# Eight graph layers on one core: batch norm folded into the next attention layer, staged stores moved between copies, a shorter last group

## What is computed

```python
def _gat_conv(x, src, dst, ea, W, a_src, a_dst, We, a_edge, bias):
    ...
    alpha = leaky_relu(al_s[s] + al_d[d] + al_e, 0.2)
    ...
    coef = ex / (denom[d] + 1e-16)
    out = segment_sum(h[s] * coef[:, None], d, num_segments=n)
    return out + bias
def _bn(x, gamma, beta):
    mu = x.mean(0)
    var = ((x - mu) ** 2).mean(0)
    return (x - mu) * rsqrt(var + EPS) * gamma + beta
```

## Time and profile before

| what | value |
|---|---|
| median of 3 runs | 9399.09 us (9398.47 to 9403.84) |
| the profiled execution's own time | 9414.12 us |
| its span in the profile | 9412.4 us |
| POOL busy | 6368.0 us, 68% of the span |
| DVE busy | 5206.9 us, 55% |
| PE busy | 4490.4 us, 48% |
| ACT busy | 1396.4 us, 15% |
| mean granted PE clock | 0.647 of full speed |
| gathers of table rows | 6272 |

### The profile page before, as it was taken

One profiled execution on the slowest core, in us unless ns is written; L12 is line 12 of the kernel. 1 busy time (PEld: TensorE's weight loads), 2 busy tenths in 40 slices (PEclk: granted clock), 3 DMA queues, 4 the chain that ended last, 5 costly groups with the idle time before them and its releaser, 6 DMA issues.

```text
span 9412.4 us, 97859 instructions
## 1 busy us (share of the span) xinstructions
PE 4490.4 (48%) x25775; PEld 3609.4 (38%) x25775; DVE 5206.9 (55%) x15729; ACT 1396.4 (15%) x2273; POOL 6368.0 (68%) x6626
## 2 busy tenths in 40 slices
PE   0655556666433344333533357254374552672533
PEld 0444433333433344333433354253352442542533
DVE  3587567777433343333433349585376763695844
ACT  1666654434200000000100020000000000100001
POOL 0777747777677767777677747777557777377774
PEclk9877777777656566555656555576655765656756
DMA  2455547776211222111211112332123321123311
GB/s 73 149 156 156 154 149 199 203 200 190 76 52 52 53 57 53 52 52 52 57 53 52 52 52 77 114 116 59 24 66 110 119 79 39 58 87 103 112 52 28
DMA packets 596438, 855.81 MB, mean 91 GB/s; under 512 B 130149, under 2 KB 400236, under 8 KB 594928
## 3 DMA queue, kind: packets, MB, share of 16 engines
q0 software_dynamic: 211680, 414.97, 17.1%
q1 hardware_dynamic: 369708, 383.31, 13.1%
q10 hardware_dynamic: 14688, 53.48, 1.4%
HBM read 654.55 MB, written 196.72 MB: 90 GB/s over the span
## 4 chain that ended last, share of the span: by engine, by line
POOL 66%; issue 23%; PE 4%; DVE 3%; SPq 1%; DMA 1%; ACT 1%; POOLq 0%; ACTq 0%; DVEq 0%
POOL rows L730 39%; POOL rows L760 23%; POOL nd L743 2%; POOL at_first L736 2%; SPq L516 1%; PE PS L1041 1%; PE PS L1015 1%; PE PS L1049 1%; DMA rows<-table,src_t 1%; POOL acc L777 0%; ACT H L817 0%; PE PS L1076 0%; PE PS L1079 0%; DMA staged<-rows 0%; DVE H L1641 0%
## 5 line engine op out<-in xcount | busy, mean ns | idle before, releaser
L730 POOL DMA_INDIRECT rows<-table,src_t x3920 | 3736.8, 953 | 1678.9 <-issue 1258.4
L1458 DVE TENSOR_TENSOR acc<-acc,PS 128x128 f32 x5488 | 1558.2, 284 | 3013.8 <-PE PS L1127 1768.8
L760 POOL DMA_INDIRECT rows<-table,src_t x2352 | 2287.7, 973 | 1129.5 <-issue 758.0
L1127 PE MATMUL PS<-onehot,rows 128*128 128x128 f32 x6272 | 1426.6, 419 | 2288.2 <-DMA rows<-table,src_t 2288.2
L1127 PEld LDWEIGHTS PS<-onehot,rows 128*128 128x128 f32 x6272 | 1320.0, 320 | 2448.2 <-DMA rows<-table,src_t 2448.2
L1158 PE MATMUL PS<-onehot,rows 128*128 128x128 f32 x3072 | 681.9, 412 | 1196.1 <-DMA rows<-table,src_t 1128.7
L1158 PEld LDWEIGHTS PS<-onehot,rows 128*128 128x128 f32 x3072 | 630.3, 313 | 1241.4 <-DMA rows<-table,src_t 1183.6
L1538 DVE TENSOR_SCALAR onehot<-PS,loc_t,shared 128x128 f32<-128x128 f32 x2352 | 943.7, 403 | 0.5
L1440 DVE TENSOR_TENSOR onehot<-PS,loc_t 128x1024 f32<-128x1024 f32 x392 | 476.8, 1217 | 0.4
L830 ACT ACTIVATE rows<-acc 128x128 f32 x343 | 77.7, 296 | 2688.5 <-DVE acc L1458 2686.4
L1231 PEld LDWEIGHTS PS<-als_bf,onehot 128*128 128x128 bf16 x7056 | 308.2, 119 | 426.5 <-DVE onehot L1712 269.6
(11 more groups left out here) (314 smaller groups left out, 5912.8 us busy)
## 6 DMA issues: line engine op xcount, KB each, us to landing
rows<-table,src_t POOLq DMA_INDIRECT x6272
staged<-rows ACTq DMA_DIRECT2D x102, 512.0 KB
H<-staged SPq DMA_DIRECT2D x102, 512.0 KB, 3.6
soft_rows<-shared SPq DMA_DIRECT2D x196, 256.0 KB
H<-soft_rows SPq DMA_DIRECT2D x98, 512.0 KB, 3.9
prod_rows<-onehot SPq DMA_DIRECT2D x98, 512.0 KB, 5.0
shared<-in_edge_weight SPq DMA_DIRECT2D x195, 256.0 KB, 3.4
G<-in_edge_attr SPq DMA_DIRECT2D x97, 512.0 KB, 6.3
```

The costliest lines, as they stand in the source:

```text
L730: pool.indirect_dma_start(rows[:, j, :], None, table[k % 2], at(src_t[:, t:t + 1]))\
L760: pool.indirect_dma_start(rows[:, g % 2 * HT + j, :], None, table[k % 2], at(src_t[:, t:t + 1]))\
L1127: last = mm(window_at(k, c, j), rows[:, r, :], onehot[:, r, :], start=True, stop=True)
L1458: tt(at, at, window_at(k, c, j), ALU.add).then_inc(added[h], 1)
```

## The change

It has three parts. **Batch norm**: the table and H get a layer's outputs without the norm, chunk by chunk as they are made. The statistics are taken after them, from transposed chunks, by DVE's batch-norm instructions, so that mean, scale and shift are columns; the scale is multiplied into the next layer's weight matrix and into the columns for al_s and al_d, and the shift times the weights is added to the next layer's bias and to al_s and al_d. In layer 7 scale and shift are spread to rows by two matmuls and applied as before. The gammas and betas are loaded as six columns in place of six rows spread over the partitions. **Staging**: the ACT queue issues the first stores between its copies, after the copies in STAGE_AFTER (-1: before the first). **The last group**: it has 6 tiles instead of 8 in every layer, and in two parts: the first four gathers signal `gathered`, the last two `gathered_end`, and PE and DVE work on the first four without waiting for the last two (in layer 1 DVE waits for both).

```diff
+RT = -(-E // P)
+LT = RT - (NG - 1) * HT
+LH = 4
+STAGE_AFTER = {5: (4, 7, 9, 11), 6: (-1, 2, 4, 6, 9, 11), 7: (-1, 2, 4, 6, 9, 11)}
...
+        def real_tiles(g):
+            return LT if g == NG - 1 else HT
+        def gather_signal(g, j):
+            return gathered_end if g == NG - 1 and j >= LH else gathered[g % 2]
...
 @gpsimd, group(l, g), and the same in gathers(i, h)
-                    for j in range(HT):
+                    for j in range(real_tiles(g)):
                         t = g * HT + j
                         pool.indirect_dma_start(rows[:, g % 2 * HT + j, :], None, table[k % 2], at(src_t[:, t:t + 1]))\
-                            .then_inc(gathered[g % 2], 16)
+                            .then_inc(gather_signal(g, j), 16)
...
 @scalar
-                    deviation(bn[:, 3 * D:4 * D], bn[:, 3 * D:4 * D])
+                    deviation(var_col, scale_col)
-                if k in GAT and 0 <= c < NCH:
-                    s.wait_ge(sum_in, (k - 5) * (NCH + 1) + c + 2)
-                    nc.scalar.activation(flat(G, c), flat(H, c), ACT.Square).then_inc(squares, 1)
+            def store_group(k, g):
+                s.wait_ge(*gathered_by(k, g))
+                s.dma_start(staged[:, g * GROUP_WORDS:(g + 1) * GROUP_WORDS],
+                            rows[:, g % 2 * HT:(g % 2 + 1) * HT, :].rearrange("p a b -> p (a b)"))\
+                    .then_inc(staged_out[g % 2], 16)
+            def copies_and_stores(k):
+                g = 0
+                for c in range(-1, NCH):
+                    if c >= 0:
+                        copy_turned(k, c)
+                    if c in STAGE_AFTER[k]:
+                        store_group(k, g)
+                        g += 1
+                for g in range(g, SG):
+                    store_group(k, g)
...
 @tensor, rows_product(k)
                 turn_rows(k, 0)
+                if k > 5:
+                    pe.wait_ge(weights_scaled, k - 5)
 to_nodes(k): first_sum and statistics (L1067 to L1081) go
                 if k in GAT:
-                    statistics(k - 5, NCH - 2)
-                    statistics(k - 5, NCH - 1)
+                    turn_outputs(k)
+            def turn_outputs(k):
+                for c in range(NCH):
+                    pe.wait_ge(h_chunks[k + 1], c + 1)
+                    wait(pe, stat_taken, (k - 5) * NCH + c - 1)
+                    for j, t in enumerate(tiles_of(c)):
+                        last = tr(stat_at(c)[:, j * D:(j + 1) * D], H3[:, t, :], ident[:])
+                    last.then_inc(stat_turned, 1)
+                pe.wait_ge(norm_known, k - 4)
+                if k < K - 1:
+                    mm(shifted_ps, shift_wide, row_matrix[k + 1], start=True, stop=True)
+                    mm(shifted_a_ps, shift_wide, gat_a[:, 2 * (k - 4):2 * (k - 3)], start=True, stop=True)\
+                        .then_inc(shift_spread, 1)
+                else:
+                    mm(scale_row_ps, scale_wide, ident[:], start=True, stop=True)
+                    mm(shift_row_ps, shift_wide, ident[:], start=True, stop=True).then_inc(shift_spread, 1)
 edge_pass(k) and weighted_pass(k)
-                    for j in range(HT):
+                    for j in range(real_tiles(c)):
+                        if c == NG - 1 and j == LH:
+                            last.then_inc(multiplied_first, 1)
+                            pe.wait_ge(*end_gathered_by(k))
...
 @vector, add_group
-                v.wait_ge(*multiplied_by(k, c))
-                for j in range(HT):
+                n = real_tiles(c)
+                if c == NG - 1:
+                    v.wait_ge(multiplied_first, turn[k] + 1)
+                else:
+                    v.wait_ge(*multiplied_by(k, c))
+                for j in range(n):
+                    if c == NG - 1 and j == LH:
+                        v.wait_ge(*multiplied_by(k, c))
...
 attention(k), for k > 5: the shifts are added as the node scalars are taken
+                    step(ts(als_n, node_scalars[:, :, 0], as_shift, None, ALU.add))
+                    step(ts(ald_n, node_scalars[:, :, 1], ad_shift, None, ALU.add))
 attention_layer(k): outputs and centred, and all of L1807 to L1835, become
+                for c in range(NCH):
+                    g = chunk(H3, c)
+                    v.wait_ge(nodes_ready, turn[k] * NCH + c + 1)
+                    step(tt(g, as_tiles(by_node(c)), per_node(rden_n, c), ALU.mult), nodes_used)
+                    step(tt(g, g, chunk(T3, c), ALU.add))
+                    step(stt(g, g, 0.01, g, ALU.mult, ALU.max), h_chunks[k + 1])
+                for c in range(NCH):
+                    v.wait_ge(stat_turned, l * NCH + c + 1)
+                    nc.vector.bn_stats(chunk_moments[:, 6 * c:6 * c + 6], stat_at(c)[:, 0:nodes_in(c)])\
+                        .then_inc(stat_taken, 1)
+                v.wait_ge(stat_taken, (l + 1) * NCH)
+                step(nc.vector.bn_aggr(fold_cols[:, 0:2], chunk_moments), var_ready)
+                inverse_taken()
+                step(recip(scale_col, scale_col))
+                step(tt(scale_col, scale_col, affine[:, 2 * l:2 * l + 1], ALU.mult))
+                step(tt(shift_col, mean_col, scale_col, ALU.mult))
+                step(tt(shift_col, affine[:, 2 * l + 1:2 * l + 2], shift_col, ALU.subtract))
+                if k == K - 1:
+                    step(copy(scale_wide, scale_col.broadcast_to([P, D])))
+                step(copy(shift_wide, shift_col.broadcast_to([P, D])), norm_known)
+                v.wait_ge(shift_spread, l + 1)
+                if k < K - 1:
+                    own, attends = row_matrix[k + 1], gat_a[:, 2 * (k - 4):2 * (k - 3)]
+                    step(ts(own, own, scale_col, None, ALU.mult))
+                    step(ts(attends, attends, scale_col, None, ALU.mult), weights_scaled)
+                    step(copy(fold_cols[:, 4:6], shifted_a_ps))
+                    step(tt(vec(bias_vec[k + 1]), vec(bias_vec[k + 1]), shifted_ps, ALU.add))
+                else:
+                    for c in range(NCH):
+                        h, x = chunk(H3, c), chunk(X3, c)
+                        wide_as = [P, len(tiles_of(c)), D]
+                        step(tt(h, h, scale_row_ps.unsqueeze(1).broadcast_to(wide_as), ALU.mult))
+                        step(tt(h, h, shift_row_ps.unsqueeze(1).broadcast_to(wide_as), ALU.add))
                         step(tt(x, x, h, ALU.add), out_ready)
```

More of the change, by code:

```diff
@@ L382, in build @@
         perm_loaded = sem("perm_loaded")
-        h_chunks = [sem(f"h_chunks{k}") for k in range(K)]
+        h_chunks = [sem(f"h_chunks{k}") for k in range(K + 1)]
         table_stored = sem("table_stored")
@@ L532, in _ @@
                 load(vec(i), vsrc[n].unsqueeze(0).broadcast_to([P, D]))
+            for l in range(3):
+                load(affine[:, 2 * l:2 * l + 1], a[f"L3_gnn_g{l + 1}"].unsqueeze(1))
+                load(affine[:, 2 * l + 1:2 * l + 2], a[f"L3_gnn_be{l + 1}"].unsqueeze(1))
             for n in msrc:
@@ L727, in gathers @@
                         wait(pool, multiplied[h], i + turn[k] * ITERS)
[L728 to L731, removed]
+                    g = 2 * i + h
+                    for j in range(real_tiles(g)):
+                        t = g * HT + j
+                        pool.indirect_dma_start(rows[:, h * HT + j, :], None, table[k % 2], at(src_t[:, t:t + 1]))\
+                            .then_inc(gather_signal(g, j), 16)
                 def scatter_firsts(l):
@@ L938, in _ @@
                     filter_pass()
+                elif k in GAT:
+                    copies_and_stores(k)
                 elif k != 1:
@@ L955, in _ @@
                 if k in GAT:
-                    for g in range(SG):
-                        s.wait_ge(*gathered_by(k, g))
-                        s.dma_start(staged[:, g * GROUP_WORDS:(g + 1) * GROUP_WORDS],
-                                    rows[:, g % 2 * HT:(g % 2 + 1) * HT, :].rearrange("p a b -> p (a b)"))\
-                            .then_inc(staged_out[g % 2], 16)
                     s.wait_ge(exp_in, k - 4)
@@ L1457, in add_group @@
                     at = acc[:, ds(first[j], D)]
-                    tt(at, at, window_at(k, c, j), ALU.add).then_inc(added[h], 1)
+                    tt(at, at, window_at(k, c, j), ALU.add).then_inc(added[h], 1 if j < n - 1 else HT - n + 1)
                     if between:
@@ L1786, in attention_layer @@
                 l = k - 5
-                minus_first, mean, square, scale, shift = (bn[:, i * D:(i + 1) * D] for i in range(5))
-                lastt = H3[:, NT - 1, :]
-                def outputs(c):
+                for c in range(NCH):
                     g = chunk(H3, c)
@@ L1857, in _ @@
                     mean_layer(k)
-CONSTS = 7
+CONSTS = 6
 LOADS = 12 + 20 + 11 + 9 + 2
```

137 lines of the change are left out of this document (53 added, 84 removed).

## The result

The changed kernel takes 9166.33 us (median of 4 runs, 9162.16 to 9170.41) against 9401.47 us (4 runs) for the kernel before: a ratio of 0.9747 with a 95% interval of 0.9733 to 0.9762, 235 us less. The forecast was 9160 us, 239 less, in a range of 9142 to 9200.

What follows compares the result with a forecast made beforehand. POOL's gathers, one every 1.25 us, were taken to bound the kernel. Savings of 20 + 31.5 + 95 + 78 + 14.4 = 239 us from the 9399.09 us median gave 9160 us, range 9142 to 9200.

Steps and rivals of the forecast that it cites:

- The short end: Last group of each pass: two gathers fewer save 20 us, splitting it in two parts saves 31.5 us.
- The folded norm: Ends of layers 5 and 6: next gather 34.8 us after the first weights matmul (S), saving 95 us.
- What became late next: Statistics and attention preparation after layers 5 and 6 come later relative to POOL, but spare room covers them: nothing charged.
- The staged stores: Start of attention layers: POOL's wait at group 2 falls to 2.2 us a layer, saving 78 us, bounds 40 and 84.
- group 0 landed + store, 11.1 against 10: At group 2: landing 3.8 us plus store 7.3 us, against group 1's 10 us of gathers, leaves a 1.1 us wait.
- Layer 7's end: First scaled chunk comes 47.6 us after the first weights matmul (S) instead of 62.0, saving 14.4 us.
- (a): Attention layers' first stores are slow or late: POOL waits about 15 us each, 9198 us; chance 0.09.
- (b): PE falls to half its clock while DVE makes the outputs, 18 us in each of three layers: 9215 us; chance 0.05.
- (c): Attention preparation ends last: first_in 50 us later in layers 6 and 7, 25 of them uncovered: 9210 us; chance 0.04.
- (d): Slower: in attention layers copies, stores and gathers queue behind each other, with stores of 40 us: 9580 us; chance 0.01.
- (e): No effect on POOL, whose gathers would wait for another thing than the table: 9379 us; chance 0.01.
- The rule against the change: DVE's two-port lock on GpSimd: folding beside POOL's gathers in layers 6 and 7 could add some 1 us.

Runs made afterwards that it cites:

- the two kernels that take it away: The changed kernel with its last group in one part: with 6 tiles 9187.62 us, with 8 tiles as before the change 9221.21 us.
- the second run of the late load: The changed kernel with SP's edge-attribute loads issued behind the picking's 98 row loads, repeated on another chip: 9178.01 us (first run, on a slower chip, 11428.31).
- fold alone: The changed kernel with a full one-part last group and all staged stores behind ACT's copies, leaving only the folded norm: 9311.69 us.
- stores 69 alone: The kernel before with only its first four staged stores per attention layer issued after ACT's copies 4, 7, 9 and 11: 9334.36 us against 9403.18.

## Why the prediction was right, and where it was not

*What bounds the kernel.* Right. Each stretch without gathers that became shorter gave its length to the end, and the pace of a gather stayed at 1.25 us.

*The short end.* Forecast 20 + 31.5 = 51.5 us, measured 54.9 by the two kernels that take it away. Landing to weights was forecast as 3.8 and is 3.80. Layer 0's end, put at 1.5, came out at 0.9, and layer 1's, put at 0, at 1.5; with the same short end layer 0's differed by up to 2 us from one execution to another.

*The folded norm.* Forecast S + 34.8 for the next gather, measured 34.4; forecast 95 us for the two layers. Their ends are 107.5 us shorter, less 10 for the short end: 97. The first output came at S + 5.49 and the last ended at S + 32.6; PE kept ahead of DVE.

*What became late next.* The weights were scaled at S + 46.0 (forecast 48), first_in came at S + 112.0 (forecast 110), and the room before the exponential is 36.66 us in layer 6 (forecast 25) and 51.65 in layer 5 (forecast 57). Uncharged, and rightly so.

*The staged stores.* Forecast 78 us, measured 84.6 - 24.8 = 60 in the traces (waits over 0.6 us counted). This is the term that was mis-sized: I left 2.2 us a layer where 7.4 to 8.8 stayed. The step that failed is "group 0 landed + store, 11.1 against 10", which took the store's 7.3 us from a stretch without the attribute load and looked at one store alone. Beside the load both halves of that sum grow: in layer 5 the store went out 5.5 us after the start of the group's last gather and took 9.2 more, 14.7 in all, and the store of group 2 did the same again. The 10 was wrong too: from the last gather of one group to the first of the group after next are nine paces, 11.25 us, so 14.7 leave 3.5, the wait in the trace, and 11.1 would have left none. None was left at these groups in the second run of the late load. I named the load and put it between 0 and 15 us; a middle value of 7 would have been nearer. That the load is the cause is what the late load shows.

*Layer 7's end.* Forecast 14.4 us and S + 47.6; measured 21.6 less 5 for the short end, 16.6, and S + 45.9.

Together 54.9 + 97 + 60 + 16.6 = 229 of the 235 us; the other 6 have no term, and are within what executions differ by. That the sum missed by only 4 us is in part luck: the stores were 18 too high, the other terms 8 too low, and the 6 came on top.

*The rivals.* (a) was half true: 8 us a layer instead of 15. (b) did not happen where I looked for it:

```profile
3429.00:3459.50 30.50, 24.36 (x196) 23.85 (x196) 23.01 (x40) 16.98 (x57) 0.00 (x0) 0.89 0.36 107
...
6697.00:6731.50 34.50, 28.03 (x209) 26.93 (x210) 27.08 (x41) 18.80 (x60) 0.00 (x0) 0.90 0.33 95
```

The clock in the outputs of layer 5 is 0.90 of full speed, as in layer 2, and it is 0.90 and 0.87 in those of layers 6 and 7. But what I had against (b), that an always busy PE is what raised the clock, does not hold: in layer 5's preparation PE was busy for all of the 45 us from 5545 on, at 0.50. So (b) was held off by the outputs as they run, and not by that reason. (c) and (d) stayed far away, as the 36.66 us show. (e) falls with the first gather at S + 34.4.

*The rule against the change.* One gather of those beside the statistics and the folding took 0.97 us, and the others 0.94 or 0.95:

```profile
6741.50 0.97 POOL L795 DMA_INDIRECT rows<-table,src_t  x1 [0.30 <-issue]
6742.77 0.94 POOL L795 DMA_INDIRECT rows<-table,src_t  x1 [0.30 <-issue]
```

The 1 us that I had worked out from the lock of the Trainium skill (SBUF — State Buffer, "SBUF: two separate sides") is not there: beside the folding's instructions, on 128 columns or fewer, a gather was at most 0.03 us longer. What costs is the large instructions, and they stayed. In each attention layer two gathers lie beside the two DVE instructions of 6.69 us that work on all of T, and not only the one that I showed; here layer 5 of the changed kernel:

```profile
6673.44 7.26 POOL L795 DMA_INDIRECT rows<-table,src_t  x1 [0.30 <-issue]
6681.01 6.42 POOL L795 DMA_INDIRECT rows<-table,src_t  x1 [0.30 <-issue]
...
6673.19 6.69 DVE L1844 TENSOR_TENSOR T<-T,small 128x6272 f32<-128x6272 f32 x1
6679.91 6.69 DVE L1845 TENSOR_TENSOR T<-T,vecs 128x6272 f32<-128x6272 f32 x1
```

The two gathers take 12 us more than two others, the same in layers 6 and 7: an estimate of 35 us of the bound engine's time that the change leaves where it was.

The order of the parts was hidden in my sum. It is right for all three together, but it gives none of them its own worth: fold alone 90, not 109; stores 69 alone and 90 beside the fold. By my sum a kernel with the fold alone would have come out 20 us too fast.

## What to carry to other kernels

When one engine's stream bounds a kernel, read the stretches in which it stands still and cost each from the last thing that it waits for; a neighbour's early start then uncovers the next wait, so cost the parts in the order in which they will stand. Take the duration of a transfer from a stretch that has the same other transfers in it, and look at the second of a chain of buffers as well as the first. A one-time load beside a stream without room has its price, here 7 to 12 us of waits a layer in both places where it was put; a place where the stream waits anyway was not tried. And a wait can hide a pause of the same engine, so taking it away may give back less than its length.

## What the runs showed of the hardware

Some 213 matmuls of the attention's preparation ran at a granted clock of 1.00 in layer 6 and 0.50 in layer 7 of one execution (2.4 and 1.2 GHz), 23 and 44 us, with PE busy throughout by the trace. Both began at the higher level, after PE had idled 2.4 and 2.8 us behind the transposes of the statistics, and both fell in the first two chunks. In layer 6 the clock had risen again by the next chunk (two matmuls of 0.78 us at 6781.90, of 0.47 at 6782.69); in layer 7 it stayed at the lower level to the end of the stretch, though PE had no gap. In the changed kernel the level is 0.50 in both layers and in layer 5, and costs nothing there, since the preparation has 36.66 us to spare or more. The Trainium skill (TensorE: Matmul & The Clock Gate, "HAM oscillation") tells of clocks lost to waits between matmuls; a busy stretch that keeps the lower level for 44 us is not its case, and no run here shows what decides between the two.

Gathers land later beside the load of the edge attributes. In layer 6, before it begins, group 0's store went out at 6742.71, 2.4 us after the start of the group's last gather (6731.52 and seven paces of 1.25). In layer 5 the load begins with the gathers, and the same store went out 5.5 us after its last gather (5544.09 and seven paces, 5558.36). With the load moved away it was 2.6 us in layer 5 as well.

After every 112 gathers of a layer, in an attention layer counted from the scatters on, POOL pauses where 0.30 us is usual: 2.0 to 2.2 us in layers 2 to 4 of both kernels, 2.0 to 4.8 in layers 0 and 1, and 2.0 to 7.7 in layers 5 to 7. What causes them no run shows.
